# The second half of an output projection moved from behind the query projection to a place between two groups of scores

## The reference

```
for each b of 16:
  h    = layernorm(x[b])                                        # 256 x 512
  q    = head_norm(h @ Wq + bq)                                 # 16 heads of 32
  k, v = head_norm(ctx[b,:240] @ Wk + bk), ctx[b,:240] @ Wv + bv
  kd,vd= the same for the last 16 context tokens, weights of their own
  a    = softmax(q k^T / sqrt(32)) v + softmax(q kd^T / sqrt(32)) vd
  x2   = x[b] + a @ Wo + bo
  out  = x2 + sum over 2 chosen experts of gate * (gelu(ln(x2) @ W1 + b1) @ W2 + b2)
```

## Time and profile before

| | us |
|---|---|
| median of 3 runs | 1132.83 (1128.11 to 1137.46) |
| the profiled execution | 1133.56 |
| its span, first to last instruction | 1131.7 |
| PE busy in the span | 968.7 |
| DVE busy | 797.6 |
| ACT busy | 638.8 |
| POOL busy | 294.9 |
| mean granted TensorE clock, share of full speed | 0.93 |

### The profile page before, as it was taken

The page is one execution under the profiler, slowest core; times in us unless marked ns, Lnnn a source line. Parts: engine busy times, 40 slices in busy tenths (PEclk is TensorE's granted clock), DMA queues, the critical chain, the costliest instruction groups (busy, mean ns, idle before and its releaser), DMA issues. The chain is left out here.

```text
span 1131.7 us, 17393 instructions
## 1 busy us (share of the span) xinstructions
PE 968.7 (86%) x5020; PEld 649.3 (57%) x5020; DVE 797.6 (70%) x1706; ACT 638.8 (56%) x1658; POOL 294.9 (26%) x203
## 2 busy tenths in 40 slices
PE   0756899999999999999999998664599999999998
PEld 0323545545555545555555555332588888888887
DVE  2736778787787787788788777334877777768774
ACT  0223887787888788778778778665322313122131
POOL 0474315315415415424414513000000000000000
PEclk9978899899999899999999999767699999999999
DMA  7015624634634634733634543676011111111110
GB/s 260 28 31 129 147 72 125 152 85 124 151 89 119 157 85 117 178 79 110 171 81 112 151 95 84 145 253 224 2 55 56 56 56 38 55 56 56 56 37 38
DMA packets 56413, 116.41 MB, mean 103 GB/s; under 512 B 13944, under 2 KB 22392, under 8 KB 56120
## 3 DMA queue, kind: packets, MB, share of 16 engines
q1 hardware_dynamic: 53760, 115.16, 37.0%
q10 hardware_dynamic: 2616, 0.79, 0.3%
HBM read 47.24 MB, written 17.30 MB: 57 GB/s over the span
## 5 line engine op out<-in xcount | busy, mean ns | idle before, releaser
L471 POOL TENSOR_TENSOR vs<-vs,neg_half 128x16 f32<-128x16 f32 x66 | 196.1, 2980 | 367.3 <-DVE vs L920 367.3
L798 ACT ACTIVATE sc<-sc,nm 128x240 f32<-128x240 f32 x512 | 222.9, 441 | 66.0 <-DVE ed L968 65.5
L963 DVE TENSOR_REDUCE pm<-sc 128x64 f32<-128x1024 f32 x128 | 156.2, 1221 | 38.2 <-PE sc L625 34.7
L578 PE MATMUL ring<-wq,xT 128*128 128x512 f32 x256 | 144.6, 718 | 21.2 <-ACT xT L766 16.1
L1388 ACT ACTIVATE hb<-hb 128x352 f32<-128x352 f32 x64 | 31.8, 497 | 227.8 <-DVE hb L1444 227.8
L625 PE MATMUL sc<-KS,QS 96*128 96x256 f32 x512 | 107.7, 335 | 44.3 <-ACT sc L798 39.4
L807 ACT ACTIVATE pt<-sc 128x1024 f32<-128x1024 f32 x128 | 124.0, 1024 | 29.4 <-PE sc L646 29.4
L625 PEld LDWEIGHTS sc<-KS,QS 96*128 96x128 f32 x512 | 75.2, 200 | 92.8 <-ACT sc L798 61.3
L591 PE MATMUL ring<-wkv,cT 128*128 128x512 f32 (+1 forms) x256 | 124.4, 611 | 0.9 <-ACT kdT L779 0.9
L678 PE MATMUL ring<-wo,ot 128*128 128x512 f32 x256 | 122.8, 604 | 0.7 <-DVE ot L1010 0.7
L798 ACT ACTIVATION_READ_ACCUMULATOR sc<-sc,nm 128x1 f32 x512 | 109.2, 213 | 0.0
(11 more groups left out here) (137 smaller groups left out, 1632.6 us busy)
## 6 DMA issues: line engine op xcount, KB each, us to landing
KS<-k_hi SPq DMA_DIRECT2D x128, 128.0 KB, 2.3
QS<-q_hi SPq DMA_DIRECT2D x128, 128.0 KB, 3.0
xin<-in_x_dram SPq DMA_DIRECT2D x16, 512.0 KB, 4.0
KS<-k_lo SPq DMA_DIRECT2D x64, 128.0 KB, 2.3
QS<-q_lo SPq DMA_DIRECT2D x64, 128.0 KB, 2.9
xres<-in_x_dram SPq DMA_DIRECT2D x16, 512.0 KB, 3.3
x_scratch<-xres SPq DMA_DIRECT2D x16, 512.0 KB, 4.7
x<-x_scratch SPq DMA_DIRECT2D x16, 512.0 KB, 3.2
```

The costliest lines, as they stand in the source:

```text
L471: pool.tensor_tensor(w, w, neg_half[0:rows, :], ALU.pow).then_inc(rstd, 1)
L578: last = pe.matmul(bank[:, :], xT[:, kc, t * P:(t + 1) * P], wq[:, kc, :], start=(kc == 0), stop=(kc == KC - 1))
L798: last = act.activation(s, s, ACT.Exp, bias=nm[:, t, h:h + 1], accum_out=den[:, t, h:h + 1])
L963: dve.tensor_reduce(pieces, s.rearrange("p h (c n) -> p h c n", n=DCA), AX_X, ALU.max, negate=True).then_inc(g_max, 1)
```

## The change

In the TensorE block alone, the four matmul instructions of `out_projection(step, b, 1, 1)` are issued between `scores(b, par, 6)` and `scores(b, par, 7)`, and no longer between `context_transposes` and `shift_transposes`. Nothing is added or removed, no semaphore changes, and no other engine's order changes.

```diff
             if attn:
                 scores(b, par, 6)
+            if wout:
+                out_projection(step, b, 1, 1)
+            if attn:
                 scores(b, par, 7)
             if proj:
                 project_q(step, b, 0)
                 context_transposes(step, b)
-            if wout:
-                out_projection(step, b, 1, 1)
             if attn:
                 shift_transposes(step, b)
```

## The result

| | before | changed |
|---|---|---|
| median of 20 runs | 1131.57 us (1128.10 to 1137.46) | 1136.07 us (1131.16 to 1144.31) |
| ratio | | **1.0043**, 95% interval 1.0025 to 1.0061 |
| the profiled execution | 1133.56 | 1134.40 |
| span | 1131.7 | 1132.0 |
| mean granted clock | 0.93 | 0.95 |

The change costs 0.4%, 4.9 us (0.0043 x 1131.6). The forecast was 1157, and its range began at 1137. The two profiled executions are only 0.8 us apart, so most of the 4.9 us lies in executions that these two traces don't show.

The account below looks back on a forecast made before the run. Each pass was taken as 28.7 us bound by TensorE plus 12.5 by ScalarE and VectorE. 1133.56 + 23 (clock falls, passes 1 to 13) + 1 (passes 14 and 15) = 1157.6, less 0.7 to the median: 1157 us, range 1137 to 1169.

Parts of the forecast that it names:

- What bounds a pass: Attention pass: 12.5 us of ScalarE and VectorE, from scores 5 to `lt`, then 28.7 of TensorE; hardly below 41.21 us.
- the 7.9 us: Time of thirteen passes above 13 x 41.21 us, put down to late `lt` transposes and clock falls, the latter almost all hidden.
- `lt` is ready before TensorE gets to it: Ahead of the shift transposes: in pass 7 `lt` is complete at 419.85, its transposes start at 420.40, behind the projection.
- The new place costs nothing, in passes 1 to 13: Between scores 6 and 7: the projection fits the idle time; scores 7 end 0.3 us later, with 0.7 us of cover.
- Full clock on query projection 0: Behind scores 7: with one idle piece of 0.85 us left, this projection runs at full clock, issued from 413.02 to 416.45.
- A hole of 3.0 us: Ahead of the shift transposes: TensorE idles from 416.9 to 419.9 in one piece, where 2.2 us in three pieces stood earlier.
- Price of a fall: Work behind the hole at half clock: a 3.4 us stretch loses 1.35 to 1.7 us, a 6.8 us one 3.15.
- I take long stretches in six passes of ten, short ones in three, none in one: Half-clock stretches from the hole in passes 1 to 13: 6.8 us long, 3.4 us short; weighted, +23 us.
- Rival 3: The fall behind the hole comes in only some passes, or so late that little is lost: 1132 to 1143 us; 9%.
- The count of pieces, six with a fall behind five: Whole trace: six idle pieces begin at full clock and last 2.4 us or more; five brought a fall, one of 2.65 none.
- The rule of the Trainium skill: On the hole: only idle gaps longer than a named length, slightly above the hole's, bring trouble; the clock would stay up.
- Passes 14 and 15, +1: No query projection there; in 14 the moved projection runs partly at half clock, scores 7 end 1.3 us later: +1 us.

Follow-up runs that it names:

- before_fill67: Kernel before with its own order, plus two unused fp32 matmuls (1.7 us) between scores 6 and 7 in passes 1 to 13: ratio 0.9965.
- hole_long: Changed kernel, query projection 0 of passes 1 to 13 without two of its eight instructions, so that the hole is 3.6 us: ratio 1.0176.
- after_again: The changed kernel itself, profiled once more: one execution of 1143.49 us.
- moved_1_13: Kernel before with the move of the change in passes 1 to 13 only, the old order in 14 and 15: ratio 1.0024.
- moved_14_15: Kernel before with the move of the change in passes 14 and 15 only: ratio 1.0018.
- fill1: Changed kernel plus one unused fp32 matmul (0.86 us) at the start of the hole in passes 1 to 13, leaving 1.89 us idle: ratio 0.9958.
- wo10_67: Kernel before with output projection (1,0) moved from between scores 4 and 5 to between scores 6 and 7: ratio 1.0045.
- wo10_56: Kernel before with output projection (1,0) moved from between scores 4 and 5 to behind the x transposes, ahead of scores 6: ratio 0.9906.
- q1_hole: Changed kernel with query projection 1 moved into the hole ahead of the shift transposes, and residual 1 behind the maxima of group 7: ratio 1.0128.

## Why the prediction was wrong, point by point

- **What bounds a pass**: right. The passes without a fall take 41.2 to 41.4 us in the changed kernel, against 41.21 read from pass 9. The clock's part of the 7.9 us was put too small, as "almost all of this is hidden": with filler alone and the projection at its old place the thirteen passes take 537.1 us, so the clock's falls cost 6.5 of it, and that "`lt` is ready before TensorE gets to it" was mostly their doing (before_fill67).
- **The new place costs nothing, in passes 1 to 13**: right. Scores 7 follow the projection without a gap, and in pass 7 VectorE went from the maxima of group 6 to those of group 7 (at 412.92) without a wait.
- **Full clock on query projection 0**: right, 3.67 to 3.70 us in all thirteen passes.
- **A hole of 3.0 us**: right in kind; the trace shows 2.75, since it counts from the end of the last transposes and not from their issue.
- **Price of a fall**: right, 1.35 to 1.8 us for a short stretch in the changed kernel's two profiles; and 44.1 to 44.2 us for a pass with a long one, where there are any (hole_long).
- **"I take long stretches in six passes of ten, short ones in three, none in one"**: wrong, and this is the step that failed. Measured: no long one, short ones in 4 or 5 of 13, none in the rest. The term was +23 us in passes 1 to 13; over these thirteen the profile of the changed kernel shows 543.2 - 543.6 = -0.4, after_again and moved_1_13 show +2.1 and +1.6, and by moved_1_13's ratio it is +2.7 in the mean. Rival 3, with falls in only some passes, had 9%, and is what happened. Two errors made the term.
  - The count of pieces, six with a fall behind five, is wrong. The trace of before has nine idle pieces of 2.4 us or more that begin at full clock, and three brought no fall. Two of these three were overlooked, and the first is the very sequence of the hole, query projection 0, context transposes, idle time, query projection 1, in the first batch of the set-up; the granted clock stayed at 1.00 from 34.6 to 57.0 us (rows below the list). Those two, the one of 2.65 us in the earlier trace rows and pieces of 2.41, 2.54 and 2.91 us (ended at 85.84, 808.65 and 101.24) are the six near the hole in length, and three of the six brought a fall. Half of thirteen, at some 1.6 us each, would have made the term 13 x 41.3 + 6.5 x 1.6 - 543.6 = +3.7. The longer pieces, up to 8.7 us, should not have been counted with them.
  - The length of the stretch was taken from pass 6. In the hole of 2.75 us no fall began more than 0.7 us before the shift transposes, and all were short; in hole_long those that began 0.8 to 0.9 us before were long, and those at 0.75 and later short. The forecast had the falls 0.7 us before to 0.3 after the shift transposes and took most of them for long; they began 0.7 before to 1.4 after.
- **The rule of the Trainium skill** ("TensorE: Matmul & The Clock Gate", "HAM oscillation — how this bites in real kernels") that I set aside was nearer to the count than I was, since in 8 or 9 passes the clock stayed up. It does not hold as a limit either: the hole, 2.75 us, was below its length and still brought falls in 4 and 5 passes.
- **Passes 14 and 15, +1**: not refuted. moved_14_15 has +2.0 with an interval from 0 to +4; the profiled execution of the changed kernel has 0.8 more behind shift transposes 14 than before, after_again 4.7.

The two overlooked pieces, TensorE in the kernel before:

```profile
39.11 3.70 PE L578 MATMUL ring<-wq,xT 128*128 128x512 f32 x8 [2.64 <-DVE q L981]
...
48.90 1.09 PE L602 MATMUL ring<-ident,q 128*128 128x128 f32 x8 [2.65 <-DVE q L926]
```

What tells a pass with a fall from its neighbour is open. The rows of both are the same up to the fall. The place of the falls relative to the shift transposes is narrow, and two executions fell in the same five passes at the same places, which speaks for something that carries over from pass to pass and against chance in each; no run here shifted the passes to test it. The whole time is open too: the profiled execution of the changed kernel is 1.7 us below its median and that of before 2.0 above, and where the slower executions lose their time is seen in one trace only, after_again.

## What to carry to other kernels

Filling an idle place moves the idle time to where the work came from: ask what work stands behind the new hole, and whether a slower clock there is hidden, before asking how much the old hole cost. Falls that lay on hidden work (thirteen, 0.5 us each) were cheaper each than those on exposed work (four, 1.6 us each), so a higher mean clock says nothing by itself. When the outcome hangs on how often something happens, list every case in the trace before you count, also those in the set-up, compare only those of like size, treat the few as the few they are, and let the range hold the whole span from never to always.

## What the runs showed of the hardware

- How often an idle piece of TensorE between dense matmuls is followed by 1.2 GHz rises with its length: 0 of 13 at 1.0 and 1.9 us (before_fill67, fill1), 4, 5 and 5 of 13 at 2.75 (changed, after_again, moved_1_13), 11 of 13 at 3.6 (hole_long), from one profiled execution each.
- Between thin groups of scores less is enough: 0.85 and 1.15 us with one such group between them brought a fall in 13 of 13 passes (before); 1.74 us ahead of a group in 9 of 13 (wo10_67); 1.0 us in 5 (wo10_56); 0.85 in none (changed, ahead of query projection 0).
- 0.69 and 2.08 us with four matmuls of keys between them brought a fall in 5 of 13 passes (q1_hole).
- 0.86 or 1.7 us of unused matmuls in a pass of 41 us raised the granted clock of the passes from 0.95 (before_fill67) or 0.98 (fill1) to 1.00, and shortened the fourteen passes by 7 us.
